# Second layer norm's statistics and the gather of picked exponentials on ScalarE, sums between the halves of the index search, residual in two buffers

## What is computed

```python
xn = (x - mu) * rsqrt(var + BN_EPS) * gamma + beta      # over all tokens
q = xn @ w_q.T                                          # 2 x 8 heads of 128
sim = einsum('pbnhd,hkpd->pbnhk', q, keys)              # 2 x 8 rows of 32 scores per token
s, i = top_k(sim, 8)
all_scores = sx[..., :, None] + sy[..., None, :]        # 64 sums per head
scores, pk = top_k(all_scores, 8)
idx = take_along_axis(ix * 32 + iy, pk)                 # 8 of 1024 experts
o = gelu(inputs . key_in[idx]) * softmax(scores)
y = sum over heads and k of o * key_out[idx]
x = layernorm(x + y)
```

## Time and profile before

| | us |
|---|---|
| median of 3 runs | 500.65 |
| lowest and highest run | 500.22, 504.22 |
| profiled execution | 502.43 |
| its span in the trace | 500.6 |

### The profile page before, as it was taken

The page is one execution under the profiler, slowest core; times in us unless marked ns, Lnnn a source line. Parts: engine busy times, 40 slices in busy tenths (PEclk is TensorE's granted clock), DMA queues, the critical chain, the costliest instruction groups (busy, mean ns, idle before and its releaser), DMA issues.

```text
span 500.6 us, 24184 instructions
## 1 busy us (share of the span) xinstructions
PE 364.9 (73%) x10097; PEld 266.1 (53%) x10097; DVE 429.3 (86%) x2691; ACT 243.7 (49%) x398; POOL 255.0 (51%) x345
## 2 busy tenths in 40 slices
PE   5979855266738787787877778778787778778755
PEld 3445542024433657375647554665467366737745
DVE  2457986999999889999999999999999999994922
ACT  2897664346324533563474437353654572344222
POOL 1023350552549465658747473769294938474600
PEclk9989956668556887887797679867987887878769
DMA  8800000000000000000000000000000000000001
GB/s 237 187 1 1 1 1 0 2 0 5 3 4 3 3 4 5 3 3 7 26 1 5 25 5 2 5 25 4 3 5 27 2 5 4 26 1 5 25 5 44
DMA packets 7662, 8.96 MB, mean 18 GB/s; under 512 B 896, under 2 KB 6912, under 8 KB 7424
## 3 DMA queue, kind: packets, MB, share of 16 engines
q1 hardware_dynamic: 6976, 7.34, 5.4%
q10 hardware_dynamic: 576, 0.07, 0.1%
HBM read 5.31 MB, written 2.10 MB: 15 GB/s over the span
## 4 chain that ended last, share of the span: by engine, by line
PE 39%; DVE 22%; issue 13%; POOL 10%; ACT 3%; ACTq 0%; DVEq 0%; POOLq 0%
PE psum L904 15%; PE psum L880 11%; PE psum L891 7%; PE psum L860 5%; DVE vals L625 4%; POOL arena L295 4%; DVE picked L658 3%; DVE idx L633 3%; DVE arena L689 3%; DVE arena L685 2%; POOL ixf L258 2%; DVE arena L682 2%; POOL code L263 1%; DVE top L639 1%; ACT arena L444 1%
## 5 line engine op out<-in xcount | busy, mean ns | idle before, releaser
L880 PE MATMUL psum<-arena 64*64 64x16 f16 x8192 | 93.6, 180 | 69.2 <-issue 60.9
L880 PEld LDWEIGHTS psum<-arena 64*64 64x64 f16 x8192 | 85.8, 116 | 87.7 <-issue 77.3
L904 PE MATMUL psum<-ko,arena 64*128 64x128 f32 x1024 | 90.4, 354 | 3.3 <-issue 3.3
L904 PEld LDWEIGHTS psum<-ko,arena 64*128 64x128 f32 x1024 | 87.0, 265 | 4.2 <-issue 3.8
L633 DVE FIND_INDEX8 idx<-vals,sims 128x8 uint32<-128x32 f32 x512 | 82.6, 186 | 0.0
L295 POOL TENSOR_TENSOR arena<-arena 128x512 f32<-128x512 f32 x60 | 77.3, 1318 | 4.8 <-ACT arena L436 4.8
L891 PE MATMUL psum<-x1T,trn 128*64 128x256 f32 x512 | 66.3, 412 | 13.8 <-ACT arena L444 13.7
L685 DVE TENSOR_TENSOR arena<-iota,listsT 128x4096 f16<-128x4096 f16 x32 | 76.3, 2385 | 0.0
L436 ACT ACTIVATE arena<-psum 128x1024 f32<-128x1024 f32 x32 | 32.6, 1018 | 67.8 <-PE psum L880 67.8
L891 PEld LDWEIGHTS psum<-x1T,trn 128*64 128x64 f32 x512 | 35.5, 148 | 51.5 <-ACT arena L444 25.8
L243 POOL TENSOR_TENSOR cand<-vals 128x128 f32<-128x128 f32 x16 | 9.4, 588 | 95.5 <-DVE vals L625 95.5
(11 more groups left out here) (118 smaller groups left out, 573.7 us busy)
## 6 DMA issues: line engine op xcount, KB each, us to landing
x<-in_L_attn_x_dram SPq DMA_DIRECT2D x8, 256.0 KB, 5.7
out_dram<-nat SPq DMA_DIRECT2D x7, 256.0 KB, 2.2
ko<-in_L_ffn_key_out_dram SPq DMA_DIRECT2D x2, 512.0 KB, 8.7
nat<-in_L_ffn_key_in_dram SPq DMA_DIRECT2D x2, 256.0 KB, 9.2
nat<-in_L_ffn_keys_dram SPq DMA_DIRECT2D x2, 128.0 KB, 5.6
out_dram<-nat SPq DMA_DIRECT2D x2, 128.0 KB, 1.7
nat<-in_L_attn_W_delta_dram SPq DMA_DIRECT2D x1, 64.0 KB, 2.9
nat<-in_L_attn_W_in_dram SPq DMA_DIRECT2D x1, 64.0 KB, 2.8
```

The costliest lines, as they stand in the source:

```text
L880: end = pe.matmul(psum[64 * e:64 * e + 64, at:at + NJ], hotx[rows, g, :, e], hotw[rows, part, g, :, e], start=(part == 0), stop=(part == 1))
L904: end = pe.matmul(y2[:, e, m % 2] if m < NS - 1 else y_last[:, e], gl[rows, m % 4, j, :], ko[rows, j, :], start=(j == 0), stop=(j == NJ - 1))
```

## The change

ScalarE gets two new pieces. `gathered(m-1)` does the copy of L665, between `exps(m)` and `convert(m-1)`. `stats2(q)` forms, for the groups `q` = 0 to 5, the sum of each of the four tiles by a copy with an accumulator output, the negative mean by a multiplication, and the sum of squared differences by a square with an accumulator output; the last two groups keep VectorE's statistics. `spread2` (the root) now follows `stats2` in the even passes, behind `signs` and `norm_out`, no longer behind the gelus of the odd ones. `norm_out` runs one pair of passes later than before, except in the tail.

On VectorE the codes stay behind the picks; the sum and the reciprocal move between the first and second half of the search for positions. `scales` moves to the odd passes. The residual alternates between two buffers.

The diff, without the replacement of `zf` by `zf_two[1]` in the functions of the tail:

```diff
@@ -128,7 +128,11 @@
         pn = arena[:, at_pn:at_pn + 3 * AW].rearrange("p (u j w) -> p u j w", u=3, j=NJ)
         at_gl = at_pn + 3 * AW
         gl = arena[:, at_gl:at_gl + 4 * AW].rearrange("p (u j w) -> p u j w", u=4, j=NJ)
-        zf = nat[:, 0:CH, :]
+        zf_two = (nat[:, 0:CH, :], nat[:, 2 * CH:3 * CH, :])
+        squares = nat[:, 3 * CH:4 * CH, :]
+        sum2 = sb("sum2", [P, CH])
+        neg2 = sb("neg2", [P, CH])
+        sq2 = sb("sq2", [P, CH])
         st2 = sb("st2", [P, CH, 6])
         mv2 = sb("mv2", [P, CH, 2])
         rstd2 = sb("rstd2", [P, CH])
...
@@ -445,17 +449,41 @@
                                    b_g[r % 2].rearrange("p (j m w) -> p j m w", j=2, m=2), ACT.Gelu).then_inc(
                                        s["gelu_done"], 1)
 
+            def gathered(m):
+                wait(act, "picked_done", m + 1)
+                wait(act, "wk_done", m)
+                act.activation(exk16, picked16[:, :, :, 0], ACT.Copy).then_inc(s["exk_done"], 1)
+
+            def stats2(q):
+                zf = zf_two[q % 2]
+                act.wait_ge(s["zf_done"], q + 1)
+                wait(act, "nmr2_done", q)
+                for t in range(CH):
+                    end = act.activation(squares[:, t, :], zf[:, t, :], ACT.Copy, accum_out=sum2[:, t:t + 1])
+                end.then_inc(s["st2_done"], 1)
+                act.wait_ge(s["st2_done"], q + 1)
+                act.mul(neg2[:, :], sum2[:, :], -1.0 / D).then_inc(s["neg2_done"], 1)
+                act.wait_ge(s["neg2_done"], q + 1)
+                for t in range(CH):
+                    end = act.activation(squares[:, t, :], zf[:, t, :], ACT.Square, bias=neg2[:, t:t + 1],
+                                         accum_out=sq2[:, t:t + 1])
+                end.then_inc(s["mv2_done"], 1)
+
             def spread2(q):
                 wait(act, "mv2_done", q + 1)
                 wait(act, "nmr2_done", q)
                 wait(act, "out_done", q)
-                act.activation(rstd2[:, :], mv2[:, :, 1], ACT.Sqrt, bias=eps[:, 0:1]).then_inc(s["sd2"], 1)
+                if q < NCH - 2:
+                    act.activation(rstd2[:, :], sq2[:, :], ACT.Sqrt, bias=eps[:, 0:1], scale=1.0 / D).then_inc(
+                        s["sd2"], 1)
+                else:
+                    act.activation(rstd2[:, :], mv2[:, :, 1], ACT.Sqrt, bias=eps[:, 0:1]).then_inc(s["sd2"], 1)
 
             def norm_out(q):
                 wait(act, "nmr2_done", q + 1)
                 wait(act, "stored", q * 16)
                 for t in range(CH):
-                    end = act.activation(outb[:, t, :], zf[:, t, :], ACT.Identity, bias=nmr2[:, t:t + 1],
+                    end = act.activation(outb[:, t, :], zf_two[q % 2][:, t, :], ACT.Identity, bias=nmr2[:, t:t + 1],
                                          scale=rstd2[:, t:t + 1])
                 end.then_inc(s["out_done"], 1)
 
...
@@ -484,6 +512,7 @@
                 if m < NS:
                     exps(m)
                 if m >= 1:
+                    gathered(m - 1)
                     convert(m - 1)
                 if m < NS:
                     low_halves(m)
...
@@ -497,15 +526,17 @@
                     normed(m + 2)
                 if m % 2 and m < NS:
                     gelus(m // 2)
-                if m >= 5 and m % 2:
-                    spread2(m // 2 - 2)
                 if m < NS and m % 2 == 0:
                     signs(m)
+                if m >= 8 and m % 2 == 0:
+                    norm_out(m // 2 - 4)
                 if m >= 6 and m % 2 == 0:
-                    norm_out(m // 2 - 3)
+                    stats2(m // 2 - 3)
+                    spread2(m // 2 - 3)
+            p_out(NS - 1, 0)
+            norm_out(NCH - 3)
+            p_out(NS - 1, 1)
             spread2(NCH - 2)
-            p_out(NS - 1, 0)
-            p_out(NS - 1, 1)
             norm_out(NCH - 2)
             for u in range(2):
                 spread2_half(u)
...
@@ -625,13 +656,13 @@
                         end = dve.max(vals[:, p, t * H + h, :], sims[:, m % 2, t, r, :])
                     end.then_inc(s["vals_done"], 1)
 
-            def indices(m):
-                for t in range(2):
-                    wait(dve, "vals_done", m * 2 + (t + 1))
-                    for r in range(ROWS):
-                        p, h = r // H, r % H
-                        end = dve.max_index(idx[:, p, t * H + h, :], vals[:, p, t * H + h, :], sims[:, m % 2, t, r, :])
-                    end.then_inc(s["idx_done"], 1)
+            def indices(m, t):
+                wait(dve, "code_done", m)
+                wait(dve, "vals_done", m * 2 + (t + 1))
+                for r in range(ROWS):
+                    p, h = r // H, r % H
+                    end = dve.max_index(idx[:, p, t * H + h, :], vals[:, p, t * H + h, :], sims[:, m % 2, t, r, :])
+                end.then_inc(s["idx_done"], 1)
 
             def top_sums(m):
                 wait(dve, "cand_done", m + 1)
...
@@ -658,15 +689,16 @@
                         end = dve.max(picked[:, w, r, :], words[:, w, r, :])
                 end.then_inc(s["picked_done"], 1)
 
-            def sums_and_codes(m):
+            def codes_of(m):
                 wait(dve, "conv_done", m)
-                wait(dve, "wlo_done", m)
                 wait(dve, "picked_done", m + 1)
-                dve.tensor_copy(exk16, picked16[:, :, :, 0]).then_inc(s["exk_done"], 1)
                 dve.tensor_tensor(codes[:, :, :], picked16[:, 0, :, 1].unsqueeze(1).to_broadcast([P, 2, 2 * SL]),
                                   masks[:, :, :].to_broadcast([P, 2, 2 * SL]), ALU.bitwise_and).then_inc(
                                       s["codes_done"], 1)
+
+            def sums_of(m):
                 wait(dve, "exk_done", m + 1)
+                wait(dve, "zs_done", m)
                 dve.reduce_sum(zsum[:, :], exk[:, :, :], AX_X).then_inc(s["z_done"], 1)
                 wait(dve, "z_done", m + 1)
                 dve.reciprocal(zinv[:, :], zsum[:, :]).then_inc(s["zinv_done"], 1)
...
@@ -692,16 +724,19 @@
                                   both.to_broadcast([P, 64, NJ, 2]), ALU.mult).then_inc(s["hot_done"], 1)
 
             def residual(q):
-                wait(dve, "out_done", q)
+                wait(dve, "out_done", q - 1)
                 wait(dve, "y2_mm", q * 2 + 2)
-                dve.tensor_tensor(zf.rearrange("p (m e) d -> p m e d", e=2), y2.rearrange("p e m d -> p m e d"),
+                dve.tensor_tensor(zf_two[q % 2].rearrange("p (m e) d -> p m e d", e=2),
+                                  y2.rearrange("p e m d -> p m e d"),
                                   x1[:, q * CH:(q + 1) * CH, :].rearrange("p (m e) d -> p m e d", e=2),
                                   ALU.add).then_inc(s["zf_done"], 1)
-                wait(dve, "zf_done", q + 1)
+
+            def stats_here(q):
+                dve.wait_ge(s["zf_done"], q + 1)
                 for t in range(CH):
-                    end = dve.bn_stats(st2[:, t, :], zf[:, t, :])
+                    end = dve.bn_stats(st2[:, t, :], zf_two[q % 2][:, t, :])
                 end.then_inc(s["st2_done"], 1)
-                wait(dve, "st2_done", q + 1)
+                dve.wait_ge(s["st2_done"], q + 1)
                 for t in range(CH):
                     end = dve.bn_aggr(mv2[:, t, :], st2[:, t, :])
                 end.then_inc(s["mv2_done"], 1)
...
@@ -710,8 +745,11 @@
                 wait(dve, "sd2", q + 1)
                 dve.reciprocal(rstd2[:, :], rstd2[:, :]).then_inc(s["rstd2_done"], 1)
                 wait(dve, "rstd2_done", q + 1)
-                dve.scalar_tensor_tensor(out=nmr2[:, :], in0=mv2[:, :, 0], scalar=-1.0, in1=rstd2[:, :],
-                                         op0=ALU.mult, op1=ALU.mult).then_inc(s["nmr2_done"], 1)
+                if q < NCH - 2:
+                    dve.tensor_tensor(nmr2[:, :], neg2[:, :], rstd2[:, :], ALU.mult).then_inc(s["nmr2_done"], 1)
+                else:
+                    dve.scalar_tensor_tensor(out=nmr2[:, :], in0=mv2[:, :, 0], scalar=-1.0, in1=rstd2[:, :],
+                                             op0=ALU.mult, op1=ALU.mult).then_inc(s["nmr2_done"], 1)
 
             for m in range(NS + 1):
                 if m < NS:
...
@@ -719,15 +757,19 @@
                 if m >= 1:
                     pack(m - 1)
                     pick(m - 1)
-                    sums_and_codes(m - 1)
+                    codes_of(m - 1)
                 if m < NS:
-                    indices(m)
+                    indices(m, 0)
+                if m >= 1:
+                    sums_of(m - 1)
+                if m < NS:
+                    indices(m, 1)
                     top_sums(m)
                 if m >= 1:
                     hots_of(m - 1, 0)
                     if m >= 5 and m % 2:
                         residual(m // 2 - 2)
-                    if m >= 6 and m % 2 == 0:
+                    if m >= 7 and m % 2:
                         scales(m // 2 - 3)
```

(13 more changed lines are left out.)

## The result

The changed kernel takes 565.42 us (median of 4 runs, 564.23 to 565.7) beside 502.02 us of the kernel before (500.22 to 504.22): ratio 1.126, 95% interval 1.120 to 1.131. It is 12.6% slower. The span of its profiled execution is 562.4 us, 61.8 more than before.

The account below looks back on a forecast made before the run. VectorE, busy 86%, was taken as the bound, with the reciprocal-weighing-`above`-signs chain just below. Odd steps 24.0 + 5.7, even steps 36.4 + 7.5 + 4.9, tail 2, less 0.4, gave 80 on 500.65: 580 us, range 532 to 598.

Parts of the forecast that it names:

- Point 1: Gather moved to ScalarE: VectorE loses 0.21 us a step, 3.4 us in all; ScalarE gains a 0.40 us copy.
- Point 2: Statistics moved to ScalarE: VectorE loses 1.3 us in each of six odd steps, 7.8 us gone.
- Point 3: ScalarE, even step: statistics and root take 5.3 us behind signs and norm_out; the picks stand 4.3 us for high_copied.
- Point 4: Exponential of odd steps: four table loads a pair instead of three, in ScalarE's free time, charged nothing.
- Point 5: Sums between search halves: reciprocal 2.3 us later, weighings begin 5.3 after the picks and meet VectorE's hots, 2.6 us a step.
- Point 6: Odd step: `above` ends 20.9 us after the picks, gelus are held, next picks end at 28.4; +4.0 us a step.
- Point 7: Even step behind it: late gather makes VectorE stand 2.3 us; step takes 32.5 us for 23.4, +9.1.
- Point 8: Two residual buffers: give nothing in the loop; in the tail, TensorE's matmuls cover the moved scales.
- rival (a): Slower without the cascade, as ScalarE and TensorE have slack; only direct prices fall due: 538 us, chance 0.25.
- for it: Argument for rival (a): in most odd steps of the kernel before, the signs are no wait of the gelus.
- the cascade: Points 6 and 7: late `above` holds signs, gelus and picks in odd steps, then scatter and gather in even ones.

Follow-up runs that it names:

- the statistics alone: Kernel before with only the statistics and root of groups 0 to 5 on ScalarE in even steps, plus two residual buffers: 515.11 us, 1.028.
- the late signs: Signs of odd steps put ahead of the seventh gelu instead of the third: changed kernel 536.8 us (1.064), kernel before 497.56 us (0.989).
- the weighing first: Changed kernel with GpSimd's weighing of step m-3 put ahead of the weights of step m-1: 517.0 us, 1.030.

## Why the prediction was right, point by point

The forecast was 580 us with a range of 532 to 598; it came to 565. The mechanism of points 5 to 7 is what the trace and the experiments show.

- *Point 1.* The gather's 3.4 us came off VectorE, but alone it costs 11 us. My price for it lay in point 7, where it belongs.
- *Point 2.* "7.8 us gone" is true of the busy time and wrong as a gain. Those operations were the gap in which GpSimd passed. Point 6 let two small operations fall behind the second one-hots, so the forecast held the effect, but I did not see that it came from point 2. That was luck. The part alone has 12 us of cost where the expectation had 0 to 9.
- *Point 3.* 5.3 us taken, 4.7 measured. The Trainium skill's figure (ScalarE: Activation LUTs, section What ACT_TABLE_LOAD costs) gave an estimate of 2.0 for the eight. Together with the small multiplication and its hand-overs they take 308.96 - 305.77 = 3.2, the eight alone 2.9; that estimate has no term for the read of the accumulator, 0.1 us or so for each. The picks of the odd steps 9 to 15 wait 3.2 to 3.8 us (2.0 in step 7), 4.3 forecast; the 4.6 us named with the experiment on the statistics alone belong to an even step.
- *Point 4.* 27 table loads in the second stage for 22, five more, and all in ScalarE's free time as said.
- *Point 5.* Weighings at +5.3, as forecast. The price was 2.6 a step; L717 and L721 show 1.0 each over the first one-hots of before, together with L714 2.1. In the even steps the weighings begin 6.9 to 8.5 us after the picks, behind the wait for the gather.
- *Point 6.* `above` at 19.8 for 20.9, picks at 27.1 for 28.4. I had added records of VectorE whole, though they overlap by some 0.08 us, and priced a passing weighing at 1.16 us where it costs 1.07. Over the seven odd steps the sum was 29.7, measured 24.2.
- *Point 7.* The sum waits 1.5 to 3.2 us for the gather (2.3 forecast). The even steps came to 38 us more than before for 48.8. The stall behind the statistics was shorter by 0.5 to 1.1 us. I had counted two whole weighings in VectorE's way in each even step, but in step 8 none stands there and in steps 6 and 14 only one does. Steps 4 and 6 came 2.1 and 1.2 us below the sum.
- *Point 8.* Nothing in the loop waits for the second buffer. The tail, put at +2, came out even (44.3 us from the last picks to the end, 44.55 before).

So three terms were too large, by 5.5, 11 and 2.2 us; with the 0.4 that steps 1 and 2 did not give back they make up the 18 us between 80 and 61.8. All three erred the same way, so none of the three hid another. Against rival (a), "for it" does not hold as written: in the kernel before the signs of odd steps wait in four of seven. Its 538 without the cascade is also near what the changed kernel with the late signs takes, 536.8, but partly by luck: its sum has no term for the gather's wait, which is 10.1 us there.

What stays open: why the late signs help the kernel before. Its trace fits the same chain, the four waits of its signs in odd steps being 7.6 us, but no run separates it from a better use of the pair of gelu buffers by TensorE. Open too are the 12 us of the statistics alone, as far as they do not come from the late `above`, and the 14 us that the changed kernel loses with the weighing first.

## What to carry to other kernels

Before work is taken off a busy engine, ask who uses the time that it fills: here a cheap one-input operation of VectorE was the gap in which GpSimd passed, and its removal cost more than it gave. And before work is put earlier on the other engine, ask what it will meet there: the weighing that left the one-hots met the codes. A value that another engine's long operations hang on must not be made late behind half a loop, even where it is itself not needed yet. And an in-order queue turns a small copy into the sum of all waits ahead of it.

## What the hardware showed that I had not expected

- A waiting GpSimd operation gets in between two of VectorE's that follow one another without a gap, and the second of VectorE's then lasts longer by most of its length. For a weighing, 1.24 us in the clear, that is 1.07 us whatever the VectorE operation: 3.35 us for 2.28, 2.29 for 1.22, 1.49 for 0.42.
- An activation with an accumulator output is two instructions on ScalarE: 0.29 to 0.40 us and 0.19 us for the read, of which each overlaps the next by about 0.1.
- TensorE's granted clock was 0.788 of full speed over the span before and 0.747 in the changed kernel, where TensorE is busy for 67% of the span and not 73%. Its experts_out matmuls took 356 instead of 354 ns, those of the scatter 184 for 180 and of the scores 1021 for 985; its busy time grew by 13.2 us. No run separates what this cost. TensorE's share of the chain that ended last fell from 39% to 19%, which speaks against it as the main loss.
